# Moving a Hadamard step and its PSUM drain behind the up matmuls of a fused attention and MLP kernel

## What is computed

```python
x = fwht(x * SU_ug) / SCALE
x_up = x @ W_up.T * (Wscale_ug[:INTER] * SCALE)
x_gate = x @ W_gate.T * (Wscale_ug[INTER:] * SCALE)
x = jax.nn.silu(x_gate) * x_up
x = fwht(x * SU_dp) / SCALE
x = x @ W_down.T * (Wscale_dp * SCALE)
```

## Time and profile before

| | us |
|---|---|
| median of 2 runs | 3474.87 (3474.04 to 3475.71) |
| the profiled execution | 3473.26 |
| its span on the slowest core (core 6) | 3472.2 |
| spans of the eight cores | 3453.1 to 3472.2 |
| TensorE busy on core 6 | 2702.8 (78% of the span) |
| VectorE, ScalarE busy | 589.2 (17%), 636.0 (18%) |
| mean granted TensorE clock, core 6 | 0.905 |

### The profile page before, as it was taken

How to read it: one execution, slowest core, us unless ns; L and a number is a source line. 1 busy time by engine, 2 the same in 40 slices (tenths; PEclk the granted TensorE clock), 3 DMA queues, 4 the chain that set the end, 5 groups by cost and what they waited for, 6 DMA issues and landing times.

```text
span 3472.2 us, 28583 instructions; the slowest of 8 cores (3453.1 to 3472.2 us)
## 1 busy us (share of the span) xinstructions
PE 2702.8 (78%) x10805; PEld 1053.2 (30%) x11024; DVE 589.2 (17%) x626; ACT 636.0 (18%) x616; POOL 114.5 (3%) x203
## 2 busy tenths in 40 slices
PE   3999976888899995117888878888787837999980
PEld 1444431222222221003333333333333313444430
DVE  0222211111111112721111111111111122000015
ACT  0000004655565565000000000000000012000010
POOL 1000000000000000000000000000000000000000
PEclk9999988999999997558999899999989978999995
DMA  9367634010100000154333333333333275554426
GB/s 153 65 105 121 119 99 102 1 37 1 37 0 1 0 1 0 43 151 80 75 61 76 61 76 63 74 62 75 70 67 69 56 160 126 113 110 110 112 54 193
DMA packets 120421, 258.76 MB, mean 75 GB/s; under 512 B 34784, under 2 KB 75744, under 8 KB 115168
## 3 DMA queue, kind: packets, MB, share of 16 engines
q0 software_dynamic: 54960, 149.54, 25.5%
q1 hardware_dynamic: 64376, 102.13, 9.2%
q10 hardware_dynamic: 952, 5.24, 0.6%
HBM read 337.19 MB, written 58.72 MB: 114 GB/s over the span
## 4 chain that ended last, share of the span: by engine, by line
PE 73%; DMA 7%; DVE 7%; ACT 6%; issue 5%; another core or an unknown queue 1%; DVEq 0%; POOL 0%; ACTq 0%; SPq 0%; POOLq 0%
PE ps_ug L164 28%; PE ps_y L164 13%; PE ps_ring L164 13%; PE ps_d L400 6%; PE ps_o L404 6%; PE ps_s L164 5%; DVE QSB L678 2%; ACT stg_b L714 2%; DMA AR<-scr_f 2%; ACT AR L457 2%; DMA ARF<-xkvA 1%; DMA ARF<-scr_f 1%; DMA out<-stg_f 1%; PE ps_rd L373 1%
## 5 line engine op out<-in xcount | busy, mean ns | idle before, releaser
L164 PE MATMUL ps_ug<-AR,QSB 128*128 128x512 bf16 x2635 | 634.2, 402 | 149.9 <-DVE QSB L678 146.6
L164 PEld LDWEIGHTS ps_ug<-AR,QSB 128*128 128x128 bf16 x2688 | 272.7, 102 | 511.3 <-issue 233.1
L164 PE MATMUL ps_ug<-AR,WBUF 128*128 128x512 bf16 x1379 | 331.3, 401 | 90.8 <-DVE QSB L678 75.5
L164 PE MATMUL ps_s<-QSB,AR 128*128 128x512 bf16 x753 | 233.8, 392 | 81.3 <-DMA AR<-scr_vt 45.9
L714 ACT ACTIVATE stg_b<-ps_ug,sgate 128x1024 bf16<-128x1024 f32 x64 | 71.3, 1114 | 1132.7 <-PE ps_ug L164 1132.7
L719 DVE SCALAR_TENSOR_TENSOR QSB<-ps_ug,scombo,stg_b 128x1024 bf16<-128x1024 f32 x64 | 82.2, 1284 | 1081.9 <-ACT stg_b L714 1081.9
L164 PE MATMUL ps_y<-ARF,QSB 128*128 128x512 bf16 x1002 | 225.3, 383 | 5.4 <-issue 4.3
L164 PEld LDWEIGHTS ps_ug<-AR,WBUF 128*128 128x128 bf16 x1408 | 142.5, 102 | 280.0 <-issue 134.2
L164 PE MATMUL ps_ring<-ARF,AR 128*128 128x512 bf16 x753 | 169.4, 383 | 54.1 <-DMA ARF<-xkvA 53.4
L400 PE MATMUL ps_d<-AR,ones_b 128*1 128x512 bf16 x512 | 197.4, 386 | 16.1 <-DVE rowbuf L419 11.2
L457 ACT ACTIVATE AR<-ps_s,biasB_sb 128x1024 bf16<-128x1024 f32 x160 | 177.9, 1112 | 116.4 <-PE ps_o L404 112.4
(11 more groups left out here) (106 smaller groups left out, 1483.8 us busy)
## 6 DMA issues: line engine op xcount, KB each, us to landing
QSB<-WdownT POOLq DMA_DIRECT2D x16, 2048.0 KB, 15.2
QSB<-WupT POOLq DMA_DIRECT2D x42, 512.0 KB, 5.1
QSB<-WgateT POOLq DMA_DIRECT2D x42, 512.0 KB, 7.6
ARF<-xkvB POOLq DMA_DIRECT2D x8, 2048.0 KB, 19.9
scr_f<-QSB SPq DMA_DIRECT2D x64, 256.0 KB, 5.4
WBUF<-WupT POOLq DMA_DIRECT2D x22, 512.0 KB, 5.1
WBUF<-WgateT POOLq DMA_DIRECT2D x22, 512.0 KB, 7.6
ARF<-xkvA POOLq DMA_DIRECT2D x4, 2048.0 KB, 41.0
```

The costliest lines, as they stand in the source:

```text
L164: return pe_.matmul(out_ap, lhsT, rhs, start=start, stop=stop, skip_group_check=True)
```

## The change

The step of one block is emitted elsewhere. Before, at the top of iteration c, the step of block c-2 was emitted (when two blocks were pending). After, the step of block c-1 is emitted between the up and the gate matmuls of iteration c. `emit_stage1` itself, its waits, the buffers and the loads are as they were. Behind the loop, `while pend` now finds one block instead of two.

```diff
                 pu, pg = PS[2 * pb], PS[2 * pb + 1]
-                if len(pend) >= 2:
-                    emit_stage1(*pend.pop(0))
                 p.w(pe_, ["ug0", "ug1", "ug2"][buf], wld[buf])
                 p.w(pe_, "dv", pu_free[pb])
                 for kc in range(KC):
...
                 p.inc(inst, "pe")
+                if pend:
+                    emit_stage1(*pend.pop(0))
                 p.w(pe_, "ac", pg_free[pb])
                 for kc in range(KC):
```

## The result

| | before | after |
|---|---|---|
| median, us | 3474.38 (8 runs) | 3170.07 (9 runs) |
| ratio of the two | | 0.9124, 95% interval 0.9114 to 0.9134 |
| span of the profiled execution | 3472.2 (core 6) | 3165.5 (core 4) |
| up/gate stage, first to last matmul into ps_ug | 1222.6 (core 6) | 917.6 (core 4) |

304 us went, 8.8%.

The account below looks back on a forecast made before the run. TensorE bounds it; its up/gate stage loses 231.3 us to stalls behind VectorE's copy and 77.2 to lower clock. Stage 911.1 + 1.3 + 3.3 = 915.7, slowest core 3166.0, + 1.1 + 1.6: 3168 us; 3155 to 3180 (80%), to 3200 (86%).

Parts of the forecast that it names:

- the sum: Up/gate stage 915.7 us; core 6 span 3472.2 - 306.9 = 3165.3, core 0 3166.0; plus 1.1 and 1.6 gives 3168.7.
- (1): TensorE, pair between up and gate: product ready after 2.9 us, up matmuls cover 6.9, slack 4.0, no stall.
- (2): Up matmuls' wait for the copy: done at about 8.8 us, needed at 14.2; 3.73 us go at 62 boundaries.
- (3): VectorE's queue delays nobody; weight loads' deadline becomes 28.5 us, where it was at least 36, at no cost.
- (4): Up/gate stage: Silu, product and copy now overlap matmuls on other PSUM banks; price zero from both sides.
- (5): Up/gate stage clock: with the gaps gone it returns from 0.93 to 1.00, gaining 76 us.
- (6): Stage's end: the 3.3 us tail of Silu, product and pair stays; 1.3 us of cold start also counted.
- A: Up/gate stage: the stall goes but the clock stays at 0.93, 3244 us, 4%; milder form up to 3198, 6%.
- B: Up/gate stage: lower clock over the long dense stretch, 3237 us at 0.93, 3396 at 0.80; 5%.
- C: Up/gate stage: mean clock below 0.75 eats the gain, 4059 us at the 1.2 GHz level throughout; 3%.
- D: Up/gate stage: the wait merely moves to the product or the weights, between 3168 and 3475 us; 2%.

Follow-up runs that it names:

- e4_cover_8: The changed kernel with the h128 pair of block c-1 after 8 of the 32 up matmuls instead of after all 32: 3259 us, ratio 0.9382.
- e5_cover_16: The changed kernel with the h128 pair of block c-1 after 16 of the 32 up matmuls: 3167.1 us, ratio 0.9118.
- e1_again: The kernel of e1_top_next, unaltered, run once more for an undisturbed profile: 3474.3 us.
- e2_copy_first: The kernel before with TensorE's order kept, but VectorE's copy of block c-2 ahead of the product of c-1: 3274 us, ratio 0.9425.
- e6_two_bufs: The changed kernel with two weight buffer pairs instead of three: ratio 0.9139.
- e3_fill_gap: The kernel before with 16 extra matmuls, results unused, behind each h128 pair: 3401.5 us, ratio 0.9792.
- e1_top_next: The kernel before, but the step emitted at the top of iteration c is that of block c-1 instead of c-2: 3482 us, ratio 1.0023.

## Why the prediction was right

3168 was forecast, 3170.07 measured, in the range and in the inner one of 3155 to 3180. That the stall and the clock loss both go, and nothing takes their place, is what the profile and the runs show. That the sum comes within 2 us is in part luck. It took all that lies outside the stage as fixed for each core. But on core 6 this was 3472.2 - 1222.6 = 2249.6 us in the profiled execution before and 3156.5 - 916.8 = 2239.7 in the one after, while on core 4 it was 2247.4 and 2247.9. Core 6 ended at 3156.5 and not at the 3165.3 of the sum; core 4, which the sum did not look at, was the slowest. Step by step:

- **(1) The product is ready after 2.9 us, slack 4.0.** Measured 2.88, and no idle time before the pair. e4_cover_8 and e5_cover_16 put the edge of the cover between 1.73 and 3.45 us, at 3.14 by the stall that is left: the product's end and 0.26 of latencies on either side, which the step had left out. Slack was 3.8. With the cover gone (e1_again) 3.14 us stood open at each block, and not 2.9, and 1.7 us of clock besides, which the step did not name.
- **(2), (3) The copy ends at 8.8 and its reader comes at 14.2.** It ended 8.9 us into the iteration, at 1718.84. e2_copy_first shows the part that the order of VectorE's queue had in it, which the prediction only argued: 2.02 of 3.73 us. The claim on the weights had a margin: landings were

```profile
DMA to landing us min/median/max: 4.9/5.1/16.3
...
DMA to landing us min/median/max: 5.0/7.1/18.2
```

  (issue to landing, us, L655 and then L656, changed kernel) against 28.5, and 14.24 was enough (e6_two_bufs).
- **(4) No price for the overlap.** 4222 matmuls in 914.1 us, less the cold start, is 0.2158 each, as in the earlier trace rows; the product stayed at 1284 ns and the copy at 1225 against 1214.
- **(5) 76 us of clock.** 73 by e3_fill_gap, where nothing but the clock changed. The prediction had the right size for this kernel, since it took the remainder of the stage and not a price for each gap. Its reading of one boundary, some eight slow matmuls after a gap, is true of 29 distances only (eight at each of 62 boundaries would be 105 us), and is not a constant that could be carried to another order: e1_top_next, whose upper end took the loss to be as before, came out 46 us above it.
- **(6) The cold start and the tail.** These were sized too small, by some 2 us. Start and end of the stage, core 4:

```profile
1579.31 16.82 PE L164 MATMUL ps_ug<-AR,WBUF 128*128 128x512 bf16 x64 [13.34 <-DMA WBUF<-WgateT]
...
1595.97 7.07 PE L164 MATMUL ps_ug<-AR,QSB 128*128 128x512 bf16 x32
```

```profile
2486.50 7.07 PE L164 MATMUL ps_ug<-AR,WBUF 128*128 128x512 bf16 x32
...
2496.55 1.01 PE L164 MATMUL ps_ug<-QSB,h 128*128 128x512 bf16 x2 [2.98 <-DVE QSB L719]
```

  16.66 us for the first 64 matmuls, 2.85 over dense where 1.33 was assumed from one core of one execution (these matmuls took 15.1 to 16.4 us on the eight cores of the kernel before, core 6 being the lowest, and 15.3 to 16.7 in the changed kernel: the cold start varies by more than 1 us from core to core); and from the slot behind gate(63), 2486.50 + 32 x 0.2158 = 2493.41, to the last matmul at 2496.9 is 3.5 against 3.3. The stage took 917.6, forecast 915.7, and these two are 1.7 of the 1.9 us between them.

Of the rivals, A (the clock stays at 0.93) is refuted by the 1.00 of the stage. B (a lower clock over a long dense stretch) did not come in the profiled execution: a dense stretch of 914 us ran at 1.00. The Trainium skill ("TensorE: Matmul & The Clock Gate", Part 1) expects 13/16 of the clock once three cores of a die run dense matmuls; the trace does not agree, with 1.00 over 914 us. C would have needed a mean below 0.75. D would have shown other waits in the place of the old ones, and there are none. Whether a limit on current exists and when it acts was not tested.

## What to carry to other kernels

When a wait names one instruction, read what stood ahead of it in its own queue: here the copy took 1.2 us, but the stall was 3.7, because the copy stood behind a product of another block that was not ready. Put a short dependent step behind work that needs none of its inputs, with at least as much cover as its chain is long (3.14 us here), and it costs no more than its own matmuls; less cover shortened the stall by its own length (1.73 us of cover, 1.73 us less). Price an idle gap of TensorE above the gap itself, and measure that price, since it was no constant: in this loop, gaps of 2.70 and 3.57 us cost about a third again in clock, gaps of 2.98 us in another order over a half again, gaps of 1.25 and 1.54 us nothing. Extra matmuls that fill the gap tell the two losses apart.

## What the runs showed of the hardware that was not expected

- The stall of e1 was shorter than that of the kernel before (3.14 against 3.73 us, idle 2.98 against 3.57) and its clock loss larger: 108 against 77 us over the stage. By the distances between products in the timeline, 22 periods of the kernel before (62 boundaries) ran at full clock throughout (17.97 us), of e1 nine of 63 (17.38 us). In e1 the pair comes behind the gap and in the kernel before ahead of it; whether that makes the difference stays open.
- Gap and clock of the stage: 1.25 us, 1.00; 1.54 us, 1.00; 2.70 us, 0.95; 3.57 us, 0.93; 2.98 us with the pair behind it, 0.91. So the loss is set by more than the length of the gap.
- Matmuls whose results nobody uses made the kernel faster: 992 of them (16 at each of 62 boundaries), by 2.1%.
